# Third attention: ScalarE takes over heads 7 to 12 from PSUM, one exponential per head

## The reference, cut to what matters

```python
qkv = bitlinear(x, w_qkv, g_qkv)              # rms norm, rounding to -128..127, ternary weights
attn = jnp.einsum('bhnd,bhmd->bhnm', q, k) * scale
attn = jax.nn.softmax(attn, axis=-1)
out = jnp.einsum('bhnm,bhmd->bhnd', attn, v)
return bitlinear(out, w_proj, g_proj)
```

## Time and profile before

| | |
|---|---|
| runs shown | 503.81, 509.16, 499.9 us, median 503.81 |
| profiled execution, span from first to last instruction | 502.6 us |
| busy of the span: PE, DVE, ACT, POOL | 71%, 48%, 24%, 16% |
| third attention, tiles 1 to 5 | 376.0 to 404.5 us |
| in it, busy: DVE, PE, ACT | 24.99, 25.13, 14.12 us |

### The profile page before, as it was taken

One profiled execution on the slowest core, in us unless ns is written; L12 is line 12 of the kernel. 1 busy time (PEld: TensorE's weight loads), 2 busy tenths in 40 slices (PEclk: granted clock), 3 DMA queues, 4 the chain that ended last, 5 costly groups with the idle time before them and its releaser, 6 DMA issues.

```text
span 502.6 us, 6588 instructions
## 1 busy us (share of the span) xinstructions
PE 358.5 (71%) x2467; PEld 289.5 (58%) x2467; DVE 242.4 (48%) x658; ACT 123.0 (24%) x349; POOL 79.2 (16%) x95
## 2 busy tenths in 40 slices
PE   0027798859799687863299999920698845999992
PEld 0027766647467455663199989920466633777771
DVE  0242670573646655445822222215859896174443
ACT  0011544001033676310032222200245411411110
POOL 0002130021333000030335444320000011000000
PEclk9999899977799679995589999975659975589998
DMA  1519400000000000080069999714600000000001
GB/s 60 147 76 228 107 0 0 3 1 0 0 1 3 0 0 2 1 221 27 16 170 258 269 256 253 187 42 123 147 0 1 1 2 0 1 1 0 2 0 36
DMA packets 23911, 33.21 MB, mean 66 GB/s; under 512 B 2416, under 2 KB 18013, under 8 KB 23878
## 3 DMA queue, kind: packets, MB, share of 16 engines
q1 hardware_dynamic: 22054, 29.03, 22.8%
q0 software_dynamic: 1824, 3.74, 2.6%
HBM read 29.98 MB, written 2.78 MB: 65 GB/s over the span
## 4 chain that ended last, share of the span: by engine, by line
PE 52%; DVE 20%; DMA 11%; issue 8%; ACT 5%; POOL 2%; SPq 0%; POOLq 0%; DVEq 0%
PE slot L531 7%; PE slot L591 6%; DMA area_c<-xs_dram,area_d 6%; PE slot L428 4%; PE slot L542 4%; PE slot L327 3%; PE slot L351 3%; DMA area_a<-patches 3%; DVE nmax L1318 3%; PE slot L365 3%; ACT area_e L1012 3%; PE slot L500 2%; PE slot L437 2%; PE slot L601 2%; DMA area_c<-ys_dram 2%
## 5 line engine op out<-in xcount | busy, mean ns | idle before, releaser
L850 POOL TENSOR_TENSOR rstd<-var_eps,half_neg 111x3 f32<-111x3 f32 x20 | 17.3, 866 | 258.3 <-DVE var_eps L1177 117.2
L591 PE MATMUL slot<-area_c,area_e 96*128 96x128 f32 x456 | 56.2, 282 | 0.0
L591 PEld LDWEIGHTS slot<-area_c,area_e 96*128 96x128 f32 x456 | 54.7, 199 | 0.1
L531 PE MATMUL slot<-x_t,area_a 96*128 96x259 f32 (+1 forms) x128 | 36.5, 440 | 0.0
L1465 DVE TENSOR_TENSOR area_c<-area_c,slot 128x384 f32<-128x384 f32 x19 | 10.5, 554 | 52.9 <-PE slot L591 52.9
L531 PEld LDWEIGHTS slot<-x_t,area_a 96*128 96x128 f32 x128 | 25.1, 202 | 10.3 <-issue 3.2
L342 PE MATMUL slot<-consts_sb,area_a 111*128 111x111 f32 x36 | 5.4, 326 | 34.8 <-DVE area_a L1186 34.8
L1012 ACT ACTIVATE area_e<-slot,nmax 111x111 f32<-111x111 f32 x72 | 24.2, 376 | 12.6 <-DVE nmax L1318 12.6
L1063 ACT ACTIVATE area_c<-slot,norm_cols_sb 96x128 f32<-96x128 f32 x38 | 11.7, 358 | 55.1 <-PE slot L580 55.1
L927 POOL DMA_INDIRECT ys_dram<-area_c,area_d x19 | 18.8, 987 | 41.0 <-DVE area_c L1472 40.6
L342 PEld LDWEIGHTS slot<-consts_sb,area_a 111*128 111x128 f32 x36 | 5.1, 184 | 34.8 <-issue 34.7
(11 more groups left out here) (234 smaller groups left out, 708.4 us busy)
## 6 DMA issues: line engine op xcount, KB each, us to landing
area_e<-w_gate_up SPq DMA_DIRECT2D x19, 576.0 KB
area_e<-w_down SPq DMA_DIRECT2D x19, 288.0 KB
area_a<-patches SPq DMA_DIRECT2D x6, 333.0 KB
area_a<-w SPq DMA_DIRECT2D x2, 864.0 KB
w_tern_sb<-w_tern SPq DMA_DIRECT2D x1, 864.0 KB, 12.3
area_b<-w SPq DMA_DIRECT2D x1, 864.0 KB
wqk_sb<-wqk SPq DMA_DIRECT2D x1, 768.0 KB, 6.4
consts_sb<-consts SPq DMA_DIRECT2D x1, 628.0 KB, 19.3
```

Of the source, the lines that this page charges most:

```text
L531: last = mm(slot[:, g, 0:live_cols(g)], w(c, part), columns[:, c, gcols(g, live_cols(g))], start=(c == 0), stop=(c == 1))
L591: last = mm(slot[:, gate_or_up, m * BLOCK:(m + 1) * BLOCK], wgu_sb[:, n % UP_SLOTS, c, at:at + 128], xb_t[:, n % 2, c, :], start=(c == 0), ...
L850: nc.gpsimd.tensor_tensor(rstd[:, norm, gt(g)], ve[:, norm, gt(g)], half_neg[:, gt(g)], ALU.pow).then_inc(S["norm_rstd"], 1)
```

## The change

Half 0 stays as it was. For half 1 DVE no longer subtracts: it multiplies the six negated maxima by the tile's scale (111x6) and increments `below_max`; ACT exponentiates the six heads one by one straight from the PSUM slot, with that product as bias and the same scale. So the slot of `score3` (t, 1) is freed by `probs` of that tile instead of `below_max`. ACT's exponentials of tile 0 stand between `scales_and_queries(0)` and `scales_and_queries(1)` now.

```diff
                 for jp in range(2):
-                    slot = take(pe, ("score3", t, jp), ("below_max", 2 * t + jp + 1))
+                    slot = take(pe, ("score3", t, jp), ("below_max", 2 * t + 1) if jp == 0 else ("probs", 2 * n + 2))
...
-            for g in range(GROUPS):
-                scales_and_queries(g)
+            def exps3(t):
+                n = TILES + t
+                act.wait_ge(S["below_max"], 2 * t + 1)
+                p = p_buf[:, (TILES + n) % PB, 0:6, :]
+                fn(p, p, ACT.Exp, scale=q_scale[:, t:t + 1]).then_inc(S["probs"], 1)
+
+                act.wait_ge(S["below_max"], 2 * t + 2)
+                for i in range(6):
+                    last = fn(p_buf[:, (TILES + n) % PB, 6 + i, :],
+                              slot_of[("score3", t, 1)][0:ROWS, i // 3, (i % 3) * ROWS:(i % 3 + 1) * ROWS], ACT.Exp,
+                              bias=nmax[:, t, 6 + i:7 + i], scale=q_scale[:, t:t + 1])
+                last.then_inc(S["probs"], 1)
+
+            scales_and_queries(0)
+            exps3(0)
+            scales_and_queries(1)
             for t in range(TILES):
-                n = TILES + t
-                for jp in range(2):
-                    act.wait_ge(S["below_max"], 2 * t + jp + 1)
-                    p = p_buf[:, (TILES + n) % PB, 6 * jp:6 * jp + 6, :]
-                    fn(p, p, ACT.Exp, scale=q_scale[:, t:t + 1]).then_inc(S["probs"], 1)
+                if t >= 1:
+                    exps3(t)
...
                     heads = slice(6 * jp, 6 * jp + 6)
+                    if jp == 1:
+
+                        v.tensor_scalar(nmax[:, t, heads], nmax[:, t, heads], q_scale[:, t:t + 1], None,
+                                        ALU.mult).then_inc(S["below_max"], 1)
+                        continue
```

## The result

The changed kernel takes 512.0 us by the median of 4 runs (509.89 to 513.3); the kernel before takes 506.49 beside it (499.9 to 511.8, 4 runs). The ratio is 1.0193, interval 1.013 to 1.0256. A second set gave 511.67 and 1.0241 (1.0114 to 1.0368). So it is slower, clear of the noise; whether by more or less than 2% these runs don't decide. The medians take in every execution, the ratios leave out those over 1.5% above the fastest of their kernel, so the two need not agree. The forecast was 512.1, but as 8.3 us on top of the 503.81 known then; by the medians here the change costs 5.5.

What follows compares the result with a forecast made beforehand. A loop closing once per tile, 5.87 us of PE's 1.35 and then DVE, was taken as the bound. Terms 3.6 + 1.8 + 1.9 + 1.0 = 8.3 us on the span gave 510.9, as median 512.1, range 506 to 518.

Steps and rivals of the forecast that it cites:

- Tile 0 and the second group (3.6): ACT copies the second group's integers behind tile 0's exponentials, so tile 1's first maximum comes 3.6 us late.
- Six exponentials (2.0): ACT's six 111x111 exponentials of a half 1 take 2.0 us together, with 1.6 and 2.6 kept as ends.
- Tiles 1 to 3 (1.8): Score slots released later by ACT's six exponentials make the first scores of tile 3 start 1.8 us later.
- the second scores of tile 2 wait: Tile 2's second scores wait for tile 1's six exponentials, starting 4.95 us behind tile 1's first maximum instead of 3.60.
- Tiles 3 to 5 (1.9): PE's turn back waits for ACT, making the tile period 6.80 us instead of 5.87; two periods cost 1.9.
- the second rival: The clock falls in PE's new pauses, 1.2 us a fall, 1.2 to 3.6 in all, 514.5 us put; chance 0.25.
- the two equal pauses of the second attention: Precedent for PE pauses of 1.84 us: eight matmuls behind one took 1.78 at a fallen clock, behind another 1.34.
- The turn of tile 5 (1.0): Behind tile 5 PE turns its probabilities at T + 5.45 instead of 4.42, 1.0 us more.
- the time of the six stands on the path six times: The six exponentials' time counts once in each of tiles 0 to 5: sum 5.9 us with 1.6, 11.9 with 2.6.
- The clock at half in tiles 2 to 5: Listed sign of being wrong: the trace after shows TensorE's clock at half in these tiles; no size given.
- six exponentials took 2.12 and not 2.6: Third rival: each small exponential on ACT costs more, 2.6 us for six, kernel at 515.7 us; chance 0.12.
- the shorter DVE loop: First rival: the slot's later release is hidden, tiles take 5.25 us, kernel at 500.1 us, not slower; chance 0.06.

Runs made afterwards that it cites:

- the other two profiles of before: Kernel before, run twice more without an edit: stage 41.9 us in both, half clock in tiles 1 to 3; single executions 500.96 and 505.76 us.
- the late pauses' profile: Changed kernel plus seven unread mask products behind the attend in tiles 4 and 5: median 510.35 us, ratio 1.0151.
- early tiles alone: The change in tiles 1 and 2 only, other tiles and ACT's order as in the kernel before: median 505.67 against 506.32 us, ratio 1.0009.
- the swapped halves: Against the kernel before, in tiles 1 to 5 ACT exponentiates heads 1 to 6 from PSUM, DVE subtracts for 7 to 12: medians 499.82, 506.58 us; ratios 1.0014, 0.9932.

## Why the prediction was right, and where only its sum was

**Tile 0 and the second group (3.6).** Right. 3.3 more against the other two profiles of before, 4.0 against the first. Moving ACT's order alone gives 2.7 to 3.4 of it; leaving tile 0 as it was takes all of it away. The 0.4 above the forecast, against the first profile, is the clock: from tile 1's first mask to its first maximum it takes 2.27 at half clock, 1.56 before, and I had put 0.2 for that.

**Six exponentials (2.0).** 2.11 to 2.12, 36 of them at 448 ns each:

```profile
L1126 ACT ACTIVATE area_e<-slot,nmax,q_scale 111x111 f32<-111x111 f32 x36 | 12.7, 448 | 2.7 <-DVE nmax L1587 2.7
```

The 2.35 estimated from the rule of the Trainium skill ("ScalarE: Activation LUTs", "Rules for kernel authors") was 0.23 above that. My row of the second attention was 0.1 below; whether the scale from a tile makes that difference no run separates. The product on DVE is 0.23, as taken.

**Tiles 1 to 3 (1.8).** The step "the second scores of tile 2 wait" failed in both profiles of the change. It needs a clock at full, as in the profile of before that I had; where the late pauses' profile has that, the wait is there, at T1 + 4.97. In the usual execution the clock is at half, PE fills these tiles alone, and the release is hidden: early tiles alone cost nothing. What the change adds there, 14.62 against 13.67 and 13.84, goes with the clock at 0.50 throughout against 0.55 and 0.54; I can't show that it is the change that holds it down, since the second profile of the swapped halves has 14.63 as well, and the changed kernel with nine products in the front 13.79.

**Tiles 3 to 5 (1.9).** The step counted two turns back held up by ACT. In both profiles of the change one is. Tile 4 to 5 is as forecast in its waits: turn back released by ACT at T + 5.06, DVE waiting, 6.8 at full clock (6.78 measured with the clock held), plus 1.3 and 1.2 because the second rival, which I gave 0.25, happens; it was priced at 1.2. Tile 3 to 4 took 7.47 and 7.58, 1.6 and 1.7 more than before, for another reason: the clock came up only in tile 3, and the release was hidden. In all 3.8, not 1.9. Of the two equal pauses of the second attention, one with a fall and one without, I took the one without as the likelier.

**The turn of tile 5 (1.0).** 0.2 and 0.3 against the other two profiles of before, in which the clock is at half there already; 2.3 against the first. The release is hidden here as well; with the clock held it shows, as 6.42 against 5.50.

**The sum.** 3.6 + 1.8 + 1.9 + 1.0 = 8.3; measured against the second profile of before 3.3 + 0.95 + 3.8 + 0.2 = 8.3. The equality is luck. That the time of the six stands on the path six times was the step behind the range, and in the change's profiles they stand there twice, in tile 0 and in tile 4; the clock made up for the rest. It was also luck for the total, since the median of before came out 2.7 us higher than the one I had started from. The clock at half in tiles 2 to 5 stood among my own signs of being wrong, and it is what the trace shows. Of the other rivals, six exponentials took 2.12 and not 2.6, and the shorter DVE loop had no part anywhere.

**What stays open.** Why the clock rose in tile 1 in the first profile of before and only late in tile 2 in two others and in tile 3 in the change, why it falls in tile 5 of the kernel before, and what sets the clock behind the stage, which alone is worth 6 us. No run here settles it.

## What to carry to other kernels

When a read of a ring's slot moves from a busy engine to an idle one, ask what comes next in that slot and what is queued behind it: here the same exponentials, with tile 0 left alone, made the stage 4.6 us longer in the half whose slot is wanted at the tile's end (0.9 of it the release, the rest at a lower clock) and nothing measurable in the half begun 1.6 us earlier. A forecast from a single profile inherits its clock; compare at least two executions stage by stage before a wait is called critical. Where TensorE is at half clock and has no gap, a later release is hidden, so ask for each wait whether it is there at both clocks. And the clock behind a pause can cost more (1.2 to 1.6 us here) than the pause's own length on the path (0.9).

## What the runs showed of the hardware

Filling a pause of PE with products that nobody reads held the clock where it was already up (late pauses: 1.2 to 1.6 us gained for each, in one profile), but nine such products in the front, where it stood at half, left it at 0.50 for the whole 12.16 us stretch, with PE busy for 10.18 of them. And one and the same kernel passes through the same four stretches in 34.5 or 41.9 us, the granted clock being what differs.

In the changed kernel PE worked without a gap from 371.44 on, and the clock rose only at some 398.3:

```profile
371.44:398.10 26.66, 26.66 (x186) 20.34 (x186) 14.19 (x21) 11.98 (x29) 0.00 (x0) 0.50 0.00 1
```

In the first profile of before it rose at about 374.9, some 5 us behind the last pause of 0.97.

Six exponentials of 111x111 from PSUM, with bias and scale from SBUF, took 2.12 us together, though each lasts 0.448: one starts every 0.33.
